# A cross-attention and feed-forward kernel: the scale of G taken from an earlier bound, the schedule written anew, and three loads issued by ScalarE

## The reference

```python
q, k, v = Wq @ layernorm(x), Wk @ ctx, Wv @ ctx          # 8 heads of 64 rows, 1024 positions
q = softmax(q, over the 64 rows of a head) * 64 ** -0.5
k = softmax(k, over the 1024 positions)
out = Wo @ (per head: (v @ k.T) @ q) + bo
x = x + out / max(norm over channels, 1e-12) * g * sqrt(128)
w = (int4 weights - zero points) * scales                 # 1024 x 1024
x = x + layernorm(x) @ w + bias
```

## Time and profile before

| | |
|---|---|
| time, median of 3 runs | 782.26 us (781.70 to 784.06) |
| the profiled execution | 783.55 us, of which 781.7 us are the span from first to last instruction |
| TensorE busy | 654.3 us, 84% |
| VectorE busy | 597.3 us, 76% |
| GpSimd busy | 510.3 us, 65% |
| ScalarE busy | 431.6 us, 55% |
| DMA engines, mean share | 42.8% |
| granted TensorE clock, mean | 0.972 of full; 1.00 from 135 to 720 us, 0.82 from 720 to 765 us |

### The profile page before, as it was taken

One profiled execution on the slowest core, in us unless ns is written; L12 is line 12 of the kernel. 1 busy time (PEld: TensorE's weight loads), 2 busy tenths in 40 slices (PEclk: granted clock), 3 DMA queues, 4 the chain that ended last, 5 costly groups with the idle time before them and its releaser, 6 DMA issues.

```text
span 781.7 us, 10910 instructions
## 1 busy us (share of the span) xinstructions
PE 654.3 (84%) x3271; PEld 418.1 (53%) x3271; DVE 597.3 (76%) x929; ACT 431.6 (55%) x676; POOL 510.3 (65%) x362
## 2 busy tenths in 40 slices
PE   2888888898898989889898889889898988989664
PEld 2655556565555656555555555555565655556231
DVE  2897768887887879787887988788788878877622
ACT  2786457475545656564565747455574755456320
POOL 3273757668585757859485785948577685866641
PEclk9989899999999999999999999999999999999796
DMA  8035263443528254352725345262625434252602
GB/s 296 27 63 127 54 155 49 113 104 68 162 54 188 44 128 97 64 150 54 188 54 159 56 82 141 51 183 54 174 42 108 119 61 114 54 135 42 141 7 81
DMA packets 180982, 78.94 MB, mean 101 GB/s; under 512 B 170440, under 2 KB 172000, under 8 KB 180960
## 3 DMA queue, kind: packets, MB, share of 16 engines
q1 hardware_dynamic: 180960, 78.68, 42.8%
HBM read 28.32 MB, written 8.39 MB: 47 GB/s over the span
## 4 chain that ended last, share of the span: by engine, by line
DVE 32%; PE 32%; issue 18%; POOL 10%; ACT 5%; DMA 1%; DVEq 1%; ACTq 0%; POOLq 0%; SPq 0%
PE ps_m L918 13%; DVE q_sum L691 6%; DVE q_nmax L679 6%; DVE k_nmax L672 5%; POOL q_exp L392 4%; DVE x2n_lo L731 3%; POOL rn L444 3%; DVE stats L753 2%; PE ps_o L1018 2%; DVE q_exp L684 2%; DVE g_lo L745 2%; PE ps_k L860 2%; ACT q_tok_hi L532 2%; PE ps_k L862 2%; PE ps_k L861 2%
## 5 line engine op out<-in xcount | busy, mean ns | idle before, releaser
L402 POOL TENSOR_TENSOR q_tok_lo<-q_exp,q_tok_hi 128x1024 f16<-128x1024 f32 x64 | 136.7, 2135 | 84.4 <-ACT q_tok_hi L532 84.4
L392 POOL TENSOR_TENSOR q_exp<-q_exp,q_rec 128x1024 f32<-128x1024 f32 x64 | 122.7, 1917 | 68.4 <-DVE q_rec L696 68.4
L521 ACT ACTIVATE q_exp<-q_exp 128x512 f32<-128x512 f32 x128 | 80.8, 631 | 150.5 <-DVE q_exp L684 150.2
L516 ACT ACTIVATE k_exp<-ps_k,k_nmax 128x1024 f32<-128x1024 f32 x64 | 71.2, 1113 | 122.4 <-DVE k_nmax L672 120.1
L918 PE MATMUL ps_m<-k_t,c_t 128*128 128x512 f32 x256 | 116.4, 598 | 0.0
L672 DVE TENSOR_REDUCE k_nmax<-ps_k 128x1 f32<-128x1024 f32 x64 | 77.9, 1217 | 39.2 <-PE ps_k L862 39.2
L971 PE MATMUL ps_m<-w_int,x_lo 128*128 128x512 f16 x240 | 93.9, 391 | 13.3 <-DMA x_lo<-x2n_lo 13.2
L679 DVE TENSOR_REDUCE q_nmax<-ps_q 128x8 f32<-128x512 f32 x128 | 86.6, 677 | 13.2 <-PE ps_q L862 13.1
L972 PE MATMUL ps_m<-w_int,x_hi 128*128 128x512 f16 x240 | 93.7, 391 | 0.0
L684 DVE TENSOR_TENSOR q_exp<-ps_q,q_nmax 128x512 f32<-128x512 f32 x128 | 88.5, 691 | 4.4
L425 POOL TENSOR_TENSOR c_lo<-c_in,c_hi 128x1024 fp32r<-128x1024 f32 x16 | 37.9, 2369 | 65.8 <-ACT c_hi L600 65.8
(11 more groups left out here) (126 smaller groups left out, 1437.5 us busy)
## 6 DMA issues: line engine op xcount, KB each, us to landing
x_in<-in_x SPq DMA_DIRECT2D x16, 512.0 KB, 5.7
c_in<-in_ctx SPq DMA_DIRECT2D x16, 512.0 KB, 6.4
x_res<-in_x SPq DMA_DIRECT2D x16, 512.0 KB, 4.9
out_x<-y SPq DMA_DIRECT2D x15, 512.0 KB, 3.4
q_hi<-q_tok_hi SPq DMA_TRANSPOSE x64, 3.1
q_lo<-q_tok_lo SPq DMA_TRANSPOSE x64, 3.0
og<-in_L_ffn_qweight SPq DMA_DIRECT2D x1, 512.0 KB, 5.3
sq<-in_L_ffn_qweight SPq DMA_DIRECT2D x1, 512.0 KB, 6.2
```

Of the source, the lines that this page charges most:

```text
L392: nc.gpsimd.tensor_tensor(pair, pair, rec.unsqueeze(2).to_broadcast([P, 2 * HEADS, DH]), ALU.mult).then_inc(qs_done, 1)
L402: nc.gpsimd.tensor_tensor(q_tok_lo[p % 2][:], q_exp[:, 2 * p:2 * p + 2, :].rearrange("p t d -> p (t d)"), q_tok_hi[p % 2][:], ALU.subtract ...
```

## The change

The scale of G is no longer taken from G but from a bound on it: the largest absolute value of the context (`c_abs`, a reduction of the whole 128x1024 context block on VectorE; `spread_c` on TensorE; `c_top` on VectorE) times that of the folded weights (`v_top`, once) times 128. It is ready an iteration before G is. So `fit_g` runs at step 5 of the iteration before, its factor is folded into `k_rec`, and VectorE writes `g_hi` and `g_lo` (now four pieces of 128 columns) straight from PSUM. `g_t`, `g_abs`, `spread_g` and ScalarE's part are gone.

The order of all engines is rewritten. TensorE projects the first quarter of K (`project_k(n, 0)`) and turns the context of the next block at the end of an iteration; `c_hi`, `c_lo` exist once instead of twice. `mix_out(0)` stands at step 1, ahead of `feed_forward(0)`, which is halved over steps 2 and 3; `mix_out(1)` is at step 4, `feed_forward(1)` at step 5, the column sums at 6 and the spreading of `rn` at 7. On ScalarE and GpSimd the second layer norm's scaling moves from the end of an iteration to the start of the next. SyncE's queue has only turning DMAs and stores; the three loads are issued by ScalarE at step 0, behind `exp_k(0)`. The diff, cut to its core:

```diff
--- before.py
+++ after.py
-G_FLOOR = 1e-25
-G_RANGE = 2.0 ** 8
+UNIT_FLOOR = 1e-30
+G_RANGE = 2.0 ** 15
...
-        c_hi = [sb(f"c_hi{s}", [P, N], F32R) for s in range(2)]
-        c_lo = [sb(f"c_lo{s}", [P, N], F32R) for s in range(2)]
+        c_hi = sb("c_hi", [P, N], F32R)
+        c_lo = sb("c_lo", [P, N], F32R)
...
# SyncE, one iteration
                     sp.dma_start_transpose(x2_hi[:], x2n_hi[:]).then_inc(x2hi_turned, 16)
+                if do_c:
+                    turn_q(c, 3, "hi")
+                if do_f:
                     sp.wait_ge(x2lo_done, f + 1)
                     sp.dma_start_transpose(x2_lo[:], x2n_lo[:]).then_inc(x2lo_turned, 16)
...
-                    sp.dma_start(x_res[:], x[c]).then_inc(xres_loaded, 16)
-                if 0 <= i < NB - 2:
-                    sp.wait_ge(xn_done, i + 1)
-                    load_x(i + 2, s)
...
-                    load_c(i + 2, s)
...
# ScalarE, one iteration
                         nc.scalar.activation(m_t[:], ps_m[:], ACT.Copy).then_inc(m_moved, 1)
...
+                    if j == 0 and do_a:
+                        exp_k(0)
+                    if j == 0 and do_c:
+                        if begun(c):
+                            act.wait_ge(x2_done, 2 * c)
+                            nc.scalar.dma_start(x_res[:], x[c]).then_inc(xres_loaded, 16)
+                    if j == 0 and (not isinstance(i, int) or 0 <= i < NB - 2):
+                        act.wait_ge(xn_done, i + 1)
+                        nc.scalar.dma_start(x_in[s][:], x[i + 2]).then_inc(x_loaded[s], 16)
+                        act.wait_ge(clo_done, i + 1)
+                        act.wait_ge(cabs_done, i + 1)
+                        act.wait_ge(tc_ready, 2 * (i + 1))
+                        nc.scalar.dma_start(c_in[s][:], ctx_in[i + 2]).then_inc(c_loaded[s], 16)
+                    if j == 0 and do_f:
...
+                        act.wait_ge(rstd2_steps, 4 * (f + 1))
...
+                        nc.scalar.activation(x2n, x2[:].rearrange("p (r t) -> p t r", t=2), ACT.Identity,
+                                             bias=nmr2[:], scale=rstd2[:], accum_out=rs2[:]).then_inc(x2n_done, 1)
...
-                        nc.scalar.activation(g_hi[:], g_t[:], ACT.Identity, scale=g_fit[:]).then_inc(ghi_done, 1)
...
# VectorE
+                def fit_g():
...
+                    dve.wait_ge(ctop_done, a + 1)
+                    nc.vector.tensor_scalar(g_unit[:], c_top[:], v_top[:], P / G_RANGE, ALU.mult,
+                                            ALU.mult).then_inc(fit_steps, 1)
...
-                        dve.wait_ge(gabs_ready, c + 1)
-                        nc.vector.tensor_reduce(g_top[:], ps_o[1][:, 0:P], op=ALU.max, axis=AX_X).then_inc(gfit_steps, 1)
...
+                        nc.vector.tensor_tensor(g_hi[:], ps_o[0][:].rearrange("p (c o) -> p c o", c=HC),
+                                                k_rec[:].unsqueeze(2).to_broadcast([P, HC, P]),
+                                                ALU.mult).then_inc(ghi_done, 1)
+                        dve.wait_ge(ghi_done, c + 1)
+                        for fc in range(HC):
+                            nc.vector.scalar_tensor_tensor(out=g_lo[:, fc, :], in0=ps_o[0][:, fc * P:(fc + 1) * P],
+                                                           scalar=k_rec[:, fc:fc + 1], in1=g_hi[:, fc, :],
+                                                           op0=ALU.mult, op1=ALU.subtract).then_inc(glo_done, 1)
...
+                        nc.vector.tensor_reduce(c_abs[:], c_in[1 - s][:], op=ALU.max, axis=AX_X,
+                                                apply_absolute_value=True).then_inc(cabs_done, 1)
...
# TensorE
+                def spread_c():
...
+                    pe.wait_ge(cabs_done, n + 1)
...
+                    nc.tensor.transpose(ps_o[1][:, 0:P], c_abs[:].to_broadcast([P, P]), ident[:]).then_inc(cabs_ready, 1)
...
                 for j in range(STEPS):
-                    if j < HC and do_a:
-                        project_k(j)
...
                     if j == 0 and do_c:
                         mix_g()
                     if j == 1 and do_c:
-                        spread_g()
-                    if j == 1 and do_f:
-                        feed_forward(0, 0, TC)
-                    if j in (2, 3) and do_c:
-                        mix_out(j - 2)
...
+                        mix_out(0)
+                    if j in (2, 3) and do_f:
+                        feed_forward(0, 4 * (j - 2), 4 * (j - 2) + 4)
+                    if j < 3 and do_a:
+                        project_k(a, j + 1)
...
+                    if j == 4 and do_c:
+                        mix_out(1)
+                    if j == 5 and do_f:
+                        feed_forward(1, 0, TC)
+                    if j == 6 and do_c:
...
+                    if j == 7 and do_n:
+                        project_k(n, 0)
+                    if j == 7 and do_a:
+                        mix_m(5, TC)
```

More of the change, by code:

```diff
@@ new lines, in iteration @@
+                    if j == 0 and do_c:
+                        high_q(c, 3)
+                    if j < 3 and do_a:
+                        exp_k(j + 1)
+                    if j in (3, 4) and do_a:
+                        move_tk(2 * (j - 1) + 1)
+                    if j == 3 and do_a:
+                        high_q(a, 0)
+                    if j == 3 and do_n:
+                        act.wait_ge(c_loaded[1 - s], loads(n, 1 - s))
+                        if begun(8 * n):
+                            act.wait_ge(k_ready, 8 * n)
+                        nc.scalar.activation(c_hi[:], c_in[1 - s][:], ACT.Copy).then_inc(chi_done, 1)
@@ L603, in iteration @@
+                    if j == 4 and do_c:
+                        squares(0)
+                        squares(1)
+                    if j == 4 and do_a:
+                        high_q(a, 1)
+                    if j in (6, 7) and do_n:
+                        move_tc(j - 6)
                     if j == 6 and do_n:
@@ new lines, in iteration @@
+                    if j == 0 and do_c:
+                        sum_q(c, 3)
+                    if j == 6 and do_f:
+                        scale_y(1)
+                    if j == 7 and do_c:
+                        for h in range(HALVES):
+                            dve.wait_ge(rb_ready, 2 * c + h + 1)
+                            dve.wait_ge(og_done, 2 * c + h + 1)
+                            nc.vector.tensor_tensor(halves(og)[h], halves(og)[h], ps_o[h][:],
+                                                    ALU.mult).then_inc(att_done, 1)
@@ L727, in iteration @@
+                    if j < 3 and do_a:
+                        if j == 2:
+                            sum_q(a, 0)
+                        max_k(a, j + 1)
                     if j == 0 and do_f:
@@ L743, in iteration @@
-                    if j == 1 and do_c:
-                        dve.wait_ge(ghi_done, c + 1)
-                        nc.vector.scalar_tensor_tensor(out=g_lo[:], in0=g_t[:], scalar=g_fit[:], in1=g_hi[:],
-                                                       op0=ALU.mult, op1=ALU.subtract).then_inc(glo_done, 1)
-                    if j == 4 and do_n:
+                    if j == 3 and do_f:
+                        if isinstance(i, int) and i == 2:
+                            dve.wait_ge(rows_moved, 6)
+                        scale_y(0)
@@ L884, in transpose_c @@
                 def transpose_c(h):
-                    if h == 0 and begun(8 * a):
-                        pe.wait_ge(tk_moved, 8 * a)
+                    pe.wait_ge(c_loaded[1 - s], loads(n, 1 - s))
+                    if isinstance(i, int) and i == FIRST:
+                        pe.wait_ge(wot_moved, 1)
+                    else:
+                        pe.wait_ge(tk_moved, 8 * n + h - 1)
                     for t in range(4):
```

425 lines of the change are left out of this document (214 added, 211 removed).

## The result

The changed kernel takes 792.0 us in the median (782.3 to 802.2), against 783.1 for the kernel before in the same rounds. The kernel is slower by about 1%, where the prediction said 757 us. Its runs differ by 20 us among themselves, those of before by 3, and on the whole the mean granted clock goes with the time: 782.3 us at 0.920, 792.0 at 0.908, 797.9 at 0.896.

A forecast was written before the change was run, and what follows sets the result against it. Bound: a chain of waits, no engine near 100%, TensorE idle 5.67 us an iteration. Start 60.0, fourteen intervals 604.8, last 39.9, end 50.4 plus 1.0, outside span 1.85: 758.0, less 1.3 to the median, 757 us; range 738 to 782.

The forecast's parts named there:

- The chain of G: From g_t to g_lo, 9.55 us through VectorE, TensorE and ScalarE; TensorE's 1.72 us wait before mix_out would go.
- `g_lo` by pieces: VectorE's four 128-column pieces from PSUM take 0.9 us in all, instead of the old g_lo's 2.11 us.
- the covered spreading of `rn`: On TensorE, mix_m covers the spreading of rn, so the 1.78 us wait before it goes.
- the last interval: The interval without a next block, given as 39.9 us by the walk.
- The walk: One new iteration followed through all engines from VectorE's sum_q(c,3): 42.8 us, plus 0.4 for hand-overs, 43.2 against 44.92.
- fourteen intervals of 43.2: Steady intervals between copies to m_t in the sum, 604.8 us together.
- `sum_q` 22.8, `x2b` behind GpSimd's `c_lo` 25.55: VectorE late in the iteration: sum_q ends at 22.8 us, x2b, held until GpSimd's c_lo ends, at 25.55.
- rival 3: GpSimd's scale_q goes ahead of VectorE's x2b, 1.9 us more, 785 us; or turned x_lo lands later, 772; chance 0.10.
- The loads: Three loads moved from SyncE to ScalarE: no gain, ScalarE's 1.7 us of issues cost 0.7 us an interval, 10 in all.
- Start and end: Ahead of the first m_t 60.0 us, with 2.5 for new reductions; behind the last 50.4 plus 1.0 for later x2n.

The follow-up runs named there:

- sums early: Changed kernel with the sixteen one-column matmuls between the two parts of feed_forward(1, ..), ahead of project_q(6): 776.5 us, ratio 0.9916.
- both moves: Changed kernel with the one-column sums between the parts of feed_forward(1, ..) and x2b at VectorE's step 2, loads on ScalarE: 763.8 us, ratio 0.9750.
- the filled wait: Changed kernel with ten 128x512 fp16 matmuls that nobody reads ahead of project_q(6), where TensorE waits for q_exp: 775.8 us, ratio 0.9915.
- the same rescue: Kernel before with the one-column sums behind feed_forward(1, 4, TC) and ten matmuls that nobody reads behind them: 809.2 us, against 830.0 without those ten.
- the sums filled: Changed kernel with a 128x512 fp16 matmul without a reader ahead of each of the eight matmul calls of the sums: 783.9 us, ratio 0.9977.
- c_lo late: Changed kernel with GpSimd's c_lo behind scale_q(a, 1) instead of ahead of it: 784.6 us, ratio 1.0013.
- `y` early: Changed kernel with sums between feed_forward(1, ..)'s parts, x2b at step 2, loads on SyncE, plus scale_y(1) ahead of gs_undo: 774.5 us, ratio 0.9888.

## Why the prediction was wrong

- The chain of G, `g_lo` by pieces, the covered spreading of `rn`: right. `g_lo` takes 1.12 us for four (0.9 said), TensorE's wait for it is 0 to 0.7 us in a steady iteration (0.3 said), none is left ahead of the spreading of `rn`, and the last interval is 39.5 us (39.9 said).
- The walk holds to 0.2 us up to `sum_q(a,1)`, which begins 21.2 us behind `sum_q(c,3)` in the walk and in the trace (357.55 - 336.33). The frame of the sum, "fourteen intervals of 43.2", is wrong for this kernel: 45.75 in the profiled execution. With the sums and `x2b` moved it is 43.3, and that it then meets 43.2 is in part luck: `x2b` costs 1.2 us in place of the walk's 2.75, and `q_rec` and `gs_undo`, held 2.0 and 1.8 us, stand in no term.
- The step that failed first is "`sum_q` 22.8, `x2b` behind GpSimd's `c_lo` 25.55". The walk took `q_rec`'s small steps to be inside `sum_q`'s 1.62 us everywhere; here one was held 1.4 us beside `c_lo`, and `sum_q` ended at 24.25. So `x2b` could not be waiting when `c_lo` ended: `q_rec` released `scale_q`, and `x2b` came 0.01 us behind it and ended at 27.3, which is rival 3's order and nearly its 1.9 us. The chance of that rival was put at 0.10, from one case in which VectorE went first. What the place of `x2b` costs an interval, clock set apart, is 0.95 us (sums early against both moves).
- The assumption that carried most weight stood in no term: full clock, since the earlier trace rows had it. The prediction took no wait of TensorE ahead of `project_q(6)` into account, and in the new order the sums stand right behind it; with `x2b` late that wait is 2.33 us. The clock that this costs is 1.4 us an interval (1.2 by the medians), shown by the filled wait and, in the kernel before, by the same rescue (1.40). It reaches the interval through the spreading of `rn`, for which VectorE waits 3.00 us. 12 x (1.4 + 0.95) = 28 of the 30.6 us; the rest is 43.39 against 43.2.
- Settled is that filling the wait, filling the sums, or moving the sums away from it keeps the clock at 1.00 in most intervals, where wait and sums together lose it in all. Why it still falls in some (five of twelve with the wait filled, two with the sums filled, two with the sums early) stays open.
- The loads: their sum was about right, 8 us by the medians, but its make-up was not. The 1.7 us on ScalarE were 0.54, and at full clock the move costs 0.06 us an interval instead of 0.7; in the changed kernel, with its low clock, it may be 0.4. One stall of 6 us in the second interval, which no term had, made most of the rest. That the move can gain nothing was right. Why SyncE's issue stands for 4.65 us there isn't settled; it did so in the four kernels with these loads on ScalarE whose second interval was 46.8 us or longer (changed, sums early, both moves, c_lo late), and in none with the loads on SyncE.
- Start and end: 60.0 was 1.6 too low, the end 2.6; neither was tested by itself.

The Trainium skill ("TensorE: Matmul & The Clock Gate", section "A second HAM failure mode: psum-queue depth-cycling") says of another kernel that short idle stretches between groups of matmuls, coming frequently, made the clock go back and forth. The trace agrees in kind, with 0.50 for 3.4 to 10.2 us of each iteration; here it is one stretch of 2.33 us an iteration, with sixteen one-column matmuls behind it. The Trainium skill ("SBUF — State Buffer", section "SBUF: two separate sides") says that of VectorE and GpSimd, where they exclude each other, whichever starts first holds the shared ports for the whole instruction. The trace agrees: GpSimd starts at 360.75, VectorE at 360.76, and `x2b` takes 2.97 us, where it takes 1.28 with GpSimd idle.

## What to carry to other kernels

A full clock in the trace before is a property of that order, not a constant: when a change moves narrow matmuls or waits of TensorE together, price both outcomes, and test with matmuls that nobody reads; put where TensorE waits anyway, they cost nothing here. In a walk through the engines, ask of every VectorE instruction on the path, one-column ones too, what GpSimd runs beside it, and put the long two-input ones where GpSimd is idle. Removing a wait can lose time if the next wait lands beside thin matmuls, as with `y` early. And a trace should be of a typical execution: where runs spread by 20 us, compare medians too before a difference of two traces is put down to a cause.

## What the runs showed of the hardware that was not expected

- Added matmuls that nobody reads made the kernel faster at four places, in both kernels: 792 to 776 (in the wait), 792 to 784 (among the sums), 768 to 751 and 830 to 809 us.
- VectorE instructions of a microsecond's fraction took 1.6 to 2.2 us beside a GpSimd instruction: `q_rec` (128x16, one tensor input) 1.58 and 2.21 beside `c_lo`, `k_rec` (128x4) 2.08 and `gs_undo` (128x1, two inputs) 1.94 beside `low_q`.
- One execution can run the same loop with the clock at 1.00 for nine iterations and at 0.96 for four: 42.8 and 44.4 us each.
- ScalarE issued a 512 KB DMA in 0.34 us (`x_in` at 337.75), beside its running activation.
- With the loads issued by ScalarE, one turning DMA's issue on SyncE took 4.65 to 4.77 us in the second interval of four of seven kernels; with the loads on SyncE it took 1.28 to 1.30 there. The cause isn't known.
